# An attention block on one core: where the row maxima of a batch are transposed, and into which accumulator bank

## The reference

```python
x = x + tanh(g_xattn) * xattn(layernorm(x), ctx, ctx, mask, Wq, Wk, Wv, Wo)
x = x + tanh(g_ffn)   * ffn(layernorm(x), w_gate, w_up, w_down, ln_weight)

# xattn: 16 query heads of 32, in 4 groups that share a key and a value head
scores = einsum('bqghd,bkgd->bghqk', Q / sqrt(32), K) + m * rel      # ALiBi slopes m
scores = where(mask, scores, neg)
w      = softmax(scores, axis=-1)
out    = einsum('bghqk,bkgd->bqghd', w, V) @ Wo
```

## Time and profile before

| what | value |
|---|---|
| median of 3 runs | 607.65 us (606.4 to 610.43) |
| the profiled execution's own time | 606.64 us |
| its span, from the first to the last instruction | 605.1 us |
| PE busy over the span | 87% |
| DVE, ACT and POOL busy | 60%, 57%, 36% |
| mean granted TensorE clock | 0.948 of full speed |

### The profile page before, as it was taken

One profiled execution on the slowest core, in us unless ns is written; L12 is line 12 of the kernel. 1 busy time (PEld: TensorE's weight loads), 2 busy tenths in 40 slices (PEclk: granted clock), 3 DMA queues, 4 the chain that ended last, 5 costly groups with the idle time before them and its releaser, 6 DMA issues.

```text
span 605.1 us, 9654 instructions
## 1 busy us (share of the span) xinstructions
PE 527.1 (87%) x3106; PEld 317.9 (53%) x3106; DVE 365.0 (60%) x671; ACT 344.5 (57%) x578; POOL 217.4 (36%) x238
## 2 busy tenths in 40 slices
PE   2499799879669899899898988788999999999994
PEld 1499799779634333344443334344555555555442
DVE  4675364245536767776566765236767676777751
ACT  2245567563225655565556555546777777777762
POOL 0010000001820373525225445025555555555540
PEclk9999999979859989999799998888999999999997
DMA  7859999999444587677757670000111111110000
GB/s 190 234 153 353 294 327 336 270 259 258 144 187 92 126 169 162 150 172 163 171 126 160 143 185 30 17 1 0 36 36 36 35 35 35 35 36 35 28 18 26
DMA packets 31338, 79.60 MB, mean 132 GB/s; under 512 B 4514, under 2 KB 17922, under 8 KB 29390
## 3 DMA queue, kind: packets, MB, share of 16 engines
q1 hardware_dynamic: 26126, 54.06, 34.5%
q0 software_dynamic: 3456, 12.58, 7.5%
q10 hardware_dynamic: 1728, 12.58, 6.6%
HBM read 57.29 MB, written 9.85 MB: 111 GB/s over the span
## 4 chain that ended last, share of the span: by engine, by line
PE 51%; DMA 17%; ACT 9%; DVE 8%; issue 7%; SPq 4%; POOL 3%; ACTq 1%; POOLq 0%; DVEq 0%
PE wide L1287 10%; PE bank L1104 9%; PE bank L1185 7%; PE wide L1104 5%; PE bank L1197 5%; PE bank L1206 4%; PE wide L1171 4%; DMA ks<-m_scratch 4%; DMA abs_b<-w_ffn 4%; DMA xt<-x 4%; PE bank L1307 3%; DMA qs<-nm_t 3%; DMA ct<-ctx_t 2%; PE bank L1143 2%; ACT yq L759 2%
## 5 line engine op out<-in xcount | busy, mean ns | idle before, releaser
L895 DVE TENSOR_REDUCE row_max<-wide 100x2 f32<-100x722 f32 x128 | 114.5, 905 | 66.9 <-PE wide L1171 66.9
L646 ACT ACTIVATE p_t<-bank 121x400 f32<-121x400 f32 x192 | 89.8, 504 | 53.0 <-PE bank L1185 50.3
L1287 PE MATMUL wide<-w_q,xq 128*128 128x512 bf16 (+1 forms) x416 | 97.4, 383 | 0.8 <-ACT xq L693 0.8
L1185 PE MATMUL bank<-qs,ks 103*121 103x400 f32 x192 | 72.4, 418 | 12.2 <-DMA qs<-nm_t 7.6
L520 POOL TENSOR_TENSOR z<-h,lnw 128x512 f32<-128x512 f32 (+1 forms) x52 | 66.6, 1282 | 30.3 <-DVE h L1015 29.9
L1171 PE MATMUL wide<-ks,qs 101*100 101x362 f32 x256 | 70.1, 360 | 6.1 <-DMA ks<-m_scratch 4.0
L1185 PEld LDWEIGHTS bank<-qs,ks 103*121 103x121 f32 x192 | 34.3, 190 | 62.7 <-ACT p_t L646 51.8
L491 POOL TENSOR_SCALAR w_q<-quant_in 128x1024 bf16<-128x1024 f32 x24 | 27.5, 1148 | 109.3 <-DMA ks<-m_scratch 108.4
L1287 PEld LDWEIGHTS wide<-w_q,xq 128*128 128x128 bf16 (+1 forms) x416 | 39.5, 99 | 48.9 <-issue 6.2
L734 ACT ACTIVATE act<-wide,small 128x512 f32<-128x512 f32 (+1 forms) x52 | 35.6, 687 | 49.8 <-PE wide L1287 38.2
L1171 PEld LDWEIGHTS wide<-ks,qs 101*100 101x100 f32 x256 | 39.7, 174 | 38.1 <-issue 28.3
(11 more groups left out here) (133 smaller groups left out, 902.6 us busy)
## 6 DMA issues: line engine op xcount, KB each, us to landing
quant_in<-w_ffn POOLq DMA_DIRECT2D x24, 512.0 KB, 4.6
ct<-ctx_t SPq DMA_DIRECT2D x16, 722.0 KB, 9.2
ks<-k_all SPq DMA_DIRECT2D x48, 181.0 KB
abs_b<-w_ffn ACTq DMA_DIRECT2D x8, 1024.0 KB, 8.2
q_scratch<-qhl SPq DMA_DIRECT2D x16, 400.0 KB, 5.1
qs<-q_scratch SPq DMA_DIRECT2D x16, 400.0 KB
abs_a<-w_ffn ACTq DMA_DIRECT2D x4, 1024.0 KB, 8.7
qs<-q_scratch SPq DMA_DIRECT2D x16, 200.0 KB
```

The costliest lines, as they stand in the source:

```text
L646: nc.scalar.activation(p_t[:, j, :], bank[j % 2][0:KT, 0:HQ], ACT.Exp).then_inc(exp_done, 1)
L895: nc.vector.tensor_reduce(row_max[:, 2 * u:2 * u + 2], wide[u % 2][0:SQ, :, 0:SK], AX_X, ALU.max).then_inc(s_maxed, 1)
L1185: nc.tensor.matmul(bank[j % 2][0:KT, 0:HQ], ks[slot][:, g, KT_AT[kt]:KT_AT[kt] + KT], qs[slot][:, g, :], start=True, stop=True).then_inc(s ...
L1287: mm = nc.tensor.matmul(wide[j % 2][0:rows, m, :], xq[:, c, 0:rows], w_q[:, m * C + c, 512 * j:512 * j + 512], start=(c == 0), stop=(c == ...
```

## The change

`turn_maxima` of batch `b` moves from the end of step `b` to step `b + 1`, behind the first pair of scores and the sums that stand behind it. It writes `bank[0]` (columns 400 to 499) in place of `wide[1]`, and so waits for the exponential that last read `bank[0]` (`exp_done`), not for ACT's copy of the maxima before. The second pair of scores doesn't wait for `nm_ready` any more. On DVE the first reduction of a step waits for the split of the batch before (`nm_split`), an order that came through PE before. After the last step `turn_maxima(15)` stands by itself.

```diff
@@ ACT @@
-                copy_high(nm_t[:, :], wide[1][0:2 * H, 0, 400:400 + SQ]).then_inc(nm_ready, 1)
+                copy_high(nm_t[:, :], bank[0][0:2 * H, 400:400 + SQ]).then_inc(nm_ready, 1)
@@ DVE @@
             def largest_scores(b, u):
                 dve.wait_ge(s_done, b * PAIRS + (u + 1))
+                if u == 0 and not (isinstance(b, int) and b == 0):
+                    dve.wait_ge(nm_split, b * 2)
@@ PE @@
-                if u == 1 and not first:
-                    pe.wait_ge(nm_ready, b)
...
             def turn_maxima(b, first=False):
                 pe.wait_ge(nm_split, b * 2 + 2)
                 if not first:
-                    pe.wait_ge(nm_ready, b)
-                nc.tensor.transpose(wide[1][0:2 * H, 0, 400:400 + SQ], nm_q[:, :].bitcast(F32), ident[0:SQ, 0:SQ]).then_inc(nm_turned, 1)
+                    pe.wait_ge(exp_done, b * UNITS - 1)
+                nc.tensor.transpose(bank[0][0:2 * H, 400:400 + SQ], nm_q[:, :].bitcast(F32), ident[0:SQ, 0:SQ]).then_inc(nm_turned, 1)
...
                     behind(b, slot, turn, u)
-                turn_maxima(b, isinstance(b, int) and b == 0)
+                    if u == 0:
+                        turn_maxima(b - 1, isinstance(b, int) and b == 1)
...
-            turn_maxima(0, True)
...
             attention_step(15, 0, 5)
+            turn_maxima(15)
```

## The result

The changed kernel is **slower**: 620.38 us in the median of 6 runs (611.02 to 629.43), beside 606.52 us for the kernel before. The ratio is 1.0196 [1.0106, 1.0285]; a second series, against its own runs of the kernel before, gave 618.89 us and 1.0284 [1.0208, 1.036]. On the 607.65 us of the prediction the first ratio is 619.6 us, 0.6 us above the upper end of the range (its interval spans 614.1 to 625.0 us), and more than double the +4.9 us that was forecast. The ratios are made from those runs of either kernel that lie within 1.5% of its fastest, so they differ from the quotients of the medians, 1.023 and 1.021.

The account below looks back on a forecast made before the run. PE with its waits, and SP's chain from the maxima copy through stores to the next loads, were taken to bound the kernel. Terms 2.1 + 2.7 + 1 - 0.6 = +5.2 us on 606.64 gave 611.8, stated as 612.5 us; range 603.5 to 619.

Parts of the forecast that it names:

- What goes: PE's waits for the split at L1214 and the second pair's for the copied maxima: about 5 us in all.
- What moves: Copy of the maxima ends 1.93 us behind the first scores; copy, stores and all loads come 1.5 us later.
- The loads' loop: Steps that the loads end last 1.93 us, T and 0.14 us: 151.0 us against 148.9 for 11 steps, +2.1 us.
- T: Time from the copy of the maxima to the next batch's loads landed; taken at 10.7 or 12.8 us by weight loads.
- The stores of the maxima: Stores issued behind POOL's weight load land at its end: a new 1.5 us stall on PE, +2.7 us in all.
- The clock: PE's granted clock falls to half after some waits; counted +1 us, from -2.5 to +5.
- Start: The 0.59 us of PE's waits ahead of step 4 go: -0.6 us.
- the clock decides: Rival: every second step stalls 1.5 us and falls, three or four falls more; 619 us or more, chance 0.17.
- the waits are simply gone: Rival: loads have room for the 1.5 us, only the gain of 3.3 + 0.8 us remains; 603.6 us, chance 0.16.
- No collision: Rival: stores of the maxima interleave with the weight load, only 2.1 - 0.6 counts; 609 us, chance 0.1.

Follow-up runs that it names:

- both profiles: Two profiled executions of the changed kernel as it is: the first took 622.25 us, the second, from the second series, 616.64 us.
- held pair: POOL's next weight load held until the stores of maxima landed, in the kernel before (593.22 us, 0.9812) and the changed kernel (619.45 us, 1.0247).
- filled kernel: Changed kernel with three throwaway matmuls put on PE ahead of each batch's wait for the stores of maxima; 615.54 us, 1.0177.
- kernel without weight loads: 22 of POOL's 24 weight loads left out, in the changed kernel (592.99 us, 0.9819) and the kernel before (605.79 us, 1.0018).

## Why the prediction was right in kind and too small

*What goes* was right: the waits of L1214 for the split are gone, and DVE's added wait and the new bank cost next to nothing (1.0 us in two places on DVE, and the 0.5 us of the bank at the last turn on PE).

*What moves* was right: the copy came 1.9 to 2.1 us behind the first scores, 1.93 in the prediction. What it didn't say is that before, the copy didn't hang on the loads of its own step at all: in a step that waits for its loads the old turn runs during the wait, so the mean of 0.4 us is no fixed place. After the change, loads, first scores, copy and next loads are one closed loop. The held pair (1.044) shows what that is worth when the loads end the steps.

*The loads' loop*, +2.1 us, was not paid in this kernel: T shrank by 0.6 to 0.7 us on the mean, to 11.1 and 11.2 where 11.65 was assumed. That the weight load gets its 4 us ahead of the loads is the likely reason; with held weight loads T is 12.6. With the shorter T the loop gives 145 us for the 11 steps, under the 148.9 of before. The waits for loads stayed at 4.5 and 5.0 us, where some 8 were forecast.

*The stores of the maxima*, +2.7 us: the mechanism was as described, landing with the end of the weight load. PE waited for them in 6 of the 11 steps in both profiles, in 3 before, so the three new places were counted well. The waits were 9.4 and 4.9 us against 2.9, that is 6.5 and 2.0 us more, on either side of the 4.5 us that three stalls of 1.5 us make. Two further places lie outside these steps.

Taken together the waits were forecast well: 2.1 + 2.7 - 0.6 = +4.2 us, and PE was idle 5.6 and 2.4 us longer over the attention. In part that is luck, with a loads' term that was too large beside a stores' term that was too small in the first profile.

*The clock*, +1 us, is **the term that was mis-sized**. The step that failed is the sentence "but PE's delay then hides under the loads' and keeps the next step off them". The new stalls were as long as those behind which the clock had fallen, as the prediction says, and it fell again: 38.8 and 17.0 us at half clock in the 11 steps in place of 10.2, and 31 and 16 us more over the attention. PE's same 1233 matmuls took 10.8 and 5.5 us longer for it. The filled kernel says that part of this does hide, since with the clock at 0.99 the median is only some 4 us less; it also has added work. So the term is at least 4 us, 7 to 8 us by the granted clocks of all runs, and 5.5 to 10.8 us as PE's busy time in the two profiles. What exactly is hidden stays open. The rival "the clock decides", at 619 us or more, came nearest to the medians of 620.4 and 618.9 us. It asked for more than four stretches of half clock between 190 and 372 us: the first profile has eight that begin in that span, the second four.

*Start*, -0.6 us, did not show: step 4 began 4.6 and 4.8 us later than before. In the first profile the steps 1 to 3 took 5.4 us longer, with 22.5 us at half clock in place of 13.4 and a new wait of 1.25 us for the stores in step 3. In the second, 3.6 us lie ahead of step 1, where the change touches nothing, and are the spread of single profiles.

The rivals: *the waits are simply gone* is refuted here, yet true of the kernel without weight loads. *No collision*, by the Trainium skill's sentence that DMAs of different engines interleave (DMA: Bandwidth & Descriptors, "Issuing engines are not separate DMA queues"), is refuted in the sense that matters: small stores issued 0.6 us behind a 512 KB load landed with its end (step 8 of the changed kernel), and behind the loads 6.6 us after their issue. The same page of the Trainium skill, in "Queues, rings and completion order", says that an engine drains a whole packet of one queue's ring before it switches. A landing at the end of the weight load would follow from that if the load is one packet on each engine, which no run here shows.

## What to carry to other kernels

A wait is worth removing only after asking what else hangs on the instruction that is moved: here one small copy released two stores and, through an in-order queue, a megabyte of loads. A producer that stands ahead of a wait for data runs during the wait; moved behind it, it closes a loop, and its whole delay is paid in each round that the loop ends. A small transfer on the critical path is best issued ahead of the large ones: holding a 512 KB load back, mostly by 1 to 3 us, until a few kilobytes had landed was worth 1.9%, more than the change meant to bring. And the waits that a profile lists are not the whole price of waiting: in both profiles here PE's own instructions grew, at the lower clock behind the waits, by twice what its idle time did.

## What the runs showed of the hardware

DVE's operations on SBUF alone, of 0.17 us, took 1.02 and 1.06 us beside POOL operations of 1.05 and 1.12 us and ended within 0.03 us of them, while its reductions out of the accumulator kept their 0.91 us beside such operations (41 of them in the kernel before without weight loads). And two nearly equal stalls need not cost the same: 1.2 us of wait ahead of step 7 in the kernel before left the clock at 1.00, 1.0 us ahead of the transposed scores of step 4 was followed by 3.5 us at 0.51, and with three matmuls put ahead of each wait for the stores the clock was at 0.99 over eleven steps.
